# Two halves of a pair side by side: a bank for each spread and each transpose, two dT buffers, and the second correction at the turn's end

## What is computed

```python
summed = segment_sum(x[src], dst);  cnt = segment_sum(ones, dst)
aggr = summed / maximum(cnt, 1.0)[:, None]
h = aggr @ W_l.T + b_l + x @ W_r.T
mu, var = mean(h, axis=0), mean(square(h - mu), axis=0)
y = x + relu((h - mu) * rsqrt(var + EPS) * gamma + beta)
out = layernorm(y, axis=-1)
```

## Time and profile before

| | |
|---|---|
| median of 3 executions | 2656.01 us (2655.27 to 2657.59) |
| the profiled execution | 2652.04 us, of which its span 2650.3 us |
| PE busy | 1762.3 us (66%) |
| DVE busy | 1970.0 us (74%) |
| ACT busy | 1466.1 us (55%) |
| POOL busy | 1412.8 us (53%) |
| DMA over the span | 753.48 MB, mean 284 GB/s |

### The profile page before, as it was taken

How to read it: one execution, slowest core, us unless ns; L and a number is a source line. 1 busy time by engine, 2 the same in 40 slices (tenths; PEclk the granted TensorE clock), 3 DMA queues, 4 the chain that set the end, 5 groups by cost and what they waited for, 6 DMA issues and landing times.

```text
span 2650.3 us, 29633 instructions
## 1 busy us (share of the span) xinstructions
PE 1762.3 (66%) x9404; PEld 1421.6 (54%) x9404; DVE 1970.0 (74%) x3465; ACT 1466.1 (55%) x2847; POOL 1412.8 (53%) x688
## 2 busy tenths in 40 slices
PE   5589999999999999999999999997310000000000
PEld 4468777888887777888887777885200000000000
DVE  7735777788887777888887777885688766666666
ACT  3224444455555444555554444543369988888887
POOL 5334554545555555455555554554276656655554
PEclk9789999999999999999999999998655555555555
DMA  4256867888877877888877778888499999999998
GB/s 149 81 159 218 276 230 230 258 257 263 262 251 248 272 257 228 264 249 265 264 245 248 251 256 247 264 253 279 127 366 426 426 426 426 426 426 416 420 420 344
DMA packets 126763, 753.48 MB, mean 284 GB/s; under 512 B 22039, under 2 KB 22039, under 8 KB 66956
## 3 DMA queue, kind: packets, MB, share of 16 engines
q1 hardware_dynamic: 72940, 619.04, 60.7%
q0 software_dynamic: 53664, 132.51, 20.0%
HBM read 515.92 MB, written 246.22 MB: 288 GB/s over the span
## 4 chain that ended last, share of the span: by engine, by line
PE 49%; DMA 26%; DVE 11%; ACT 7%; issue 4%; POOL 2%; SPq 1%; DVEq 0%; POOLq 0%; ACTq 0%
DMA out<-hx 19%; PE pd L533 10%; PE pd L535 10%; PE pd L534 10%; PE pz L638 4%; PE pz L640 4%; PE pz L639 4%; DMA xf<-x,gi 4%; ACT hx L876 3%; ACT hx L886 2%; DVE x_lo L1032 2%; PE px L632 2%; DMA hs<-h_scratch 2%; DVE hot L1038 1%; PE pe L624 1%
## 5 line engine op out<-in xcount | busy, mean ns | idle before, releaser
L1368 POOL DMA_INDIRECT h_scratch<-zz,si x156 | 306.4, 1964 | 683.5 <-ACT zz L790 467.8
L533 PE MATMUL pd<-wc_hi,x_hi 128*128 128x512 f32 x1564 | 639.1, 409 | 40.8 <-POOL x_lo L1295 24.6
L534 PE MATMUL pd<-wc_lo,x_hi 128*128 128x512 f32 x1564 | 617.6, 395 | 7.0 <-issue 7.0
L535 PE MATMUL pd<-wc_hi,x_lo 128*128 128x512 f32 x1564 | 619.1, 396 | 0.0
L1391 POOL TENSOR_TENSOR hx<-hx,scale_b 128x2560 f32<-128x2560 f32 (+2 forms) x91 | 439.5, 4843 | 291.5 <-DMA hx<-h_scratch 250.0
L745 ACT ACTIVATE h_out<-pd 128x512 f32<-128x512 f32 x391 | 233.0, 596 | 403.5 <-PE pd L535 401.9
L533 PEld LDWEIGHTS pd<-wc_hi,x_hi 128*128 128x128 f32 x1564 | 298.3, 191 | 102.4 <-POOL x_lo L1295 24.6
L1320 POOL DMA_INDIRECT xn<-x,gi x156 | 310.3, 1989 | 47.7 <-issue 44.9
L534 PEld LDWEIGHTS pd<-wc_lo,x_hi 128*128 128x128 f32 x1564 | 298.8, 191 | 63.8 <-issue 7.3
L535 PEld LDWEIGHTS pd<-wc_hi,x_lo 128*128 128x128 f32 x1564 | 297.7, 190 | 66.0
L783 ACT ACTIVATE dT_hi<-px 128x512 fp32r<-128x512 f32 x156 | 93.3, 598 | 399.3 <-PE px L632 388.0
(11 more groups left out here) (214 smaller groups left out, 2939.3 us busy)
## 6 DMA issues: line engine op xcount, KB each, us to landing
raw<-xT_whole SPq DMA_DIRECT2D x78, 1280.0 KB
h_scratch<-h_out SPq DMA_DIRECT2D x78, 1280.0 KB
hs<-h_scratch SPq DMA_DIRECT2D x78, 1280.0 KB
hx<-x SPq DMA_DIRECT2D x78, 1280.0 KB, 20.6
hx<-h_scratch SPq DMA_DIRECT2D x77, 1280.0 KB, 15.4
out<-hx SPq DMA_DIRECT2D x77, 1280.0 KB, 18.1
xn<-x,gi POOLq DMA_INDIRECT x156
xf<-x,gi POOLq DMA_INDIRECT x156
```

What stands on the lines that cost most here:

```text
L533: pe.matmul(pd[i][0:n, :], hi, wc["hi"][:, kc, :], start=kc == 0, stop=False)
L534: pe.matmul(pd[i][0:n, :], hi, wc["lo"][:, kc, :], start=False, stop=False)
L535: last = pe.matmul(pd[i][0:n, :], lo, wc["hi"][:, kc, :], start=False, stop=kc == KC - 1)
L1368: pool.indirect_dma_start(out=h_dram[:, :], out_offset=by, in_=zz[:, h, :], in_offset=None, bounds_check=N + 2 * P - 1, oob_is_err=True, c ...
```

## The change

- The spread of half 1 goes to the bank `p6` and its transposes to `p7` (`spread_to`, `turned`); half 0 keeps `pe_` and `px`. `dT_hi` and `dT_lo` are there twice.
- The waits on what frees a bank or buffer now reach two halves back instead of one (`2 * u + h - 1` for `2 * u + h`, from pair 1 on). `correction` and `copy_z` keep theirs, since `pz` stays single.
- In PE's list both spreads, then both transposes, then both corrections stand together, spaced by tiles: the second correction is last in the turn, behind the fifth tile.
- ACT's list: `copy_z(u, 1)` stands at the head of the next turn; the copy of the fifth tile is in its own turn and not at the head of the next; the two `difference_high` stand behind the second and the third tile's copy; `copy_z(u, 0)` stands behind `extras_high`.
- DVE's list: both differences ahead of the squares, both `difference_low` behind them; `x_low` has five gaps instead of four. With t = 2 as the third tile of a turn it stood at the turn's end and now stands ahead of `take_sums`; as the fourth it stays at the end; as the fifth it stood behind `difference_low(p, 0)` of the next turn and now behind `difference(p, 0)`.

The number of instructions of each engine is the same.

```diff
         acc2 = sr("acc2", [P, TG, D], F32)
         hs = sr("hs", [P, 2, TG, D], F32)
-        dT_hi = sr("dT_hi", [P, KC, P], F32R)
-        dT_lo = sr("dT_lo", [P, KC, P], F32R)
+        dT_hi = [sr(f"dT_hi{h}", [P, KC, P], F32R) for h in range(2)]
+        dT_lo = [sr(f"dT_lo{h}", [P, KC, P], F32R) for h in range(2)]
...
         pe_, px, pz, psl, p6, p7 = (ps(n) for n in ("pe", "px", "pz", "psl", "p6", "p7"))
         banks = [(pe_, px), (pz, psl), (p6, p7)]
+
+        spread_to, turned = (pe_, p6), (px, p7)
         turn = [pe_, px, pz, psl, *pd]
...
                     pe.wait_ge(s_xel, u + 1)
                     pe.wait_ge(s_spread, u + 1)
-                if 2 * u + h > 0:
-                    pe.wait_ge(s_d, 2 * u + h)
+                if u > 0:
+                    pe.wait_ge(s_d, 2 * u + h - 1)
                 to = spread[:, h * P:(h + 1) * P]
-                pe.matmul(pe_[:], to, xe_hi[:], start=True, stop=False)
-                pe.matmul(pe_[:], to, xe_lo[:], start=False, stop=True).then_inc(s_e, 1)
+                pe.matmul(spread_to[h][:], to, xe_hi[:], start=True, stop=False)
+                pe.matmul(spread_to[h][:], to, xe_lo[:], start=False, stop=True).then_inc(s_e, 1)
             def transpose_difference(u, h):
                 pe.wait_ge(s_d, 2 * u + h + 1)
-                if 2 * u + h > 0:
-                    pe.wait_ge(s_dl, 2 * u + h)
+                if u > 0:
+                    pe.wait_ge(s_dl, 2 * u + h - 1)
                 for kc in range(KC):
-                    last = pe.transpose(px[:, kc * P:(kc + 1) * P], dd[:, h, kc * P:(kc + 1) * P], ident[:])
+                    last = pe.transpose(turned[h][:, kc * P:(kc + 1) * P], dd[:, h, kc * P:(kc + 1) * P], ident[:])
                 last.then_inc(s_x, 1)
-            def times_wl(out_bank, n):
+            def times_wl(out_bank, n, h=0):
                 for kc in range(KC):
-                    hi, lo = dT_hi[:, kc, 0:n], dT_lo[:, kc, 0:n]
+                    hi, lo = dT_hi[h][:, kc, 0:n], dT_lo[h][:, kc, 0:n]
                     pe.matmul(out_bank[0:n, :], hi, wl["hi"][:, kc, :], start=kc == 0, stop=False)
                     pe.matmul(out_bank[0:n, :], hi, wl["lo"][:, kc, :], start=False, stop=False)
...
                 if 2 * u + h > 0:
                     pe.wait_ge(s_ze, 2 * u + h)
-                times_wl(pz, P).then_inc(s_z, 1)
+                times_wl(pz, P, h).then_inc(s_z, 1)
             def sum_columns(m, acc, tiles):
...
                     plain(0)
                     if a is not None:
-                        transpose_difference(a, 0)
+                        spread_extras(a, 1)
                     plain(1)
                     if a is not None:
-                        correction(a, 0)
-                        spread_extras(a, 1)
+                        transpose_difference(a, 0)
                     plain(2)
                     if a is not None:
...
                     plain(3)
                     if a is not None:
-                        correction(a, 1)
+                        correction(a, 0)
+                    plain(4)
                     if u + 2 < U:
                         fill_slots(u + 2)
-                    plain(4)
+                    if a is not None:
+                        correction(a, 1)
                 pe.wait_ge(s_a1, G)
                 sum_columns(0, acc1, range(1, TG))
...
             def difference_high(u, h):
                 act.wait_ge(s_x, 2 * u + h + 1)
-                if 2 * u + h > 0:
-                    act.wait_ge(s_z, 2 * u + h)
-                act.activation(dT_hi[:].rearrange("p c r -> p (c r)"), px[:], ACT.Copy).then_inc(s_dh, 1)
+                if u > 0:
+                    act.wait_ge(s_z, 2 * u + h - 1)
+                act.activation(dT_hi[h][:].rearrange("p c r -> p (c r)"), turned[h][:], ACT.Copy).then_inc(s_dh, 1)
             def copy_z(u, h):
...
                                     x_high(g + 1, (g + 1) % 2, kc)
-                    plain(tiles_at(u - 1)[TG - 1:])
+                    if pair_at(u - 1) is not None:
+                        copy_z(u - 1, 1)
                     if sp_ is not None:
                         for t in range(3, tiles_in(sp_)):
                             square(sp_, t)
+                    plain(tiles[0:2])
                     if a is not None:
                         difference_high(a, 0)
-                    plain(tiles[0:2])
+                    plain(tiles[2:3])
+                    if a is not None:
+                        difference_high(a, 1)
+                    plain(tiles[3:4])
+                    if pair_at(u + 1) is not None:
+                        extras_high(u + 1)
                     if a is not None:
                         copy_z(a, 0)
-                        difference_high(a, 1)
-                    plain(tiles[2:4])
-                    if pair_at(u + 1) is not None:
-                        extras_high(u + 1)
+                    plain(tiles[4:])
                     if s is not None:
                         for t in range(min(3, tiles_in(s))):
                             square(s, t)
-                    if a is not None:
-                        copy_z(a, 1)
             act.wait_ge(s_bs, 1)
...
                 if u > 0:
                     dve.wait_ge(s_x, 2 * u + h - 1)
-                dve.tensor_tensor(dd[:, h, :], pe_[:], xf[:, u % 2, h, :], ALU.add).then_inc(s_d, 1)
+                dve.tensor_tensor(dd[:, h, :], spread_to[h][:], xf[:, u % 2, h, :], ALU.add).then_inc(s_d, 1)
             def difference_low(u, h):
                 dve.wait_ge(s_dh, 2 * u + h + 1)
-                if 2 * u + h > 0:
-                    dve.wait_ge(s_z, 2 * u + h)
-                dve.tensor_tensor(dT_lo[:].rearrange("p c r -> p (c r)"), px[:],
-                                  dT_hi[:].rearrange("p c r -> p (c r)").bitcast(F32), ALU.subtract).then_inc(s_dl, 1)
+                if u > 0:
+                    dve.wait_ge(s_z, 2 * u + h - 1)
+                dve.tensor_tensor(dT_lo[h][:].rearrange("p c r -> p (c r)"), turned[h][:],
+                                  dT_hi[h][:].rearrange("p c r -> p (c r)").bitcast(F32), ALU.subtract).then_inc(s_dl, 1)
             def take_sums(g):
...
                 for u in turns():
                     p = pair_at(u)
-                    low = lows(u, ((0, 1), (0, 2), (0, 3), (0, 3), (1, 0)))
+                    low = lows(u, ((0, 1), (0, 2), (0, 3), (0, 4), (1, 0)))
                     def x_lows(place):
...
                     if p is not None:
                         difference(p, 0)
+                    x_lows(0)
                     if 0 <= u + 2 < U:
                         one_hots(u + 2)
                     if p is not None:
-                        difference_low(p, 0)
-                    x_lows(0)
+                        difference(p, 1)
+                    x_lows(1)
                     if sums_at(u - 1) is not None:
                         take_squares(sums_at(u - 1))
-                    x_lows(1)
                     if p is not None:
-                        difference(p, 1)
+                        difference_low(p, 0)
                     x_lows(2)
                     if p is not None:
                         difference_low(p, 1)
+                    x_lows(3)
                     if sums_at(u) is not None:
                         take_sums(sums_at(u))
...
                         begin(u + 1, 0)
                         begin(u + 1, 1)
-                    x_lows(3)
+                    x_lows(4)
                     if 0 <= u + 2 < U:
                         indices(u + 2)
```

More of the change, by code:

```diff
@@ L817, in correct @@
                             act.wait_ge(s_c[5], TG * g + t)
-                        act.activation(dT_hi[:, :, 0:n], px[:].rearrange("p (c r) -> p c r", c=KC)[:, :, 0:n],
+                        act.activation(dT_hi[0][:, :, 0:n], px[:].rearrange("p (c r) -> p c r", c=KC)[:, :, 0:n],
                                        ACT.Copy).then_inc(s_c[3], 1)
@@ L1155, in correct @@
                         dve.wait_ge(s_c[3], TG * g + t + 1)
-                        dve.tensor_tensor(dT_lo[:, :, 0:m], px[:].rearrange("p (c r) -> p c r", c=KC)[:, :, 0:m],
-                                          dT_hi[:, :, 0:m].bitcast(F32), ALU.subtract).then_inc(s_c[4], 1)
+                        dve.tensor_tensor(dT_lo[0][:, :, 0:m], px[:].rearrange("p (c r) -> p c r", c=KC)[:, :, 0:m],
+                                          dT_hi[0][:, :, 0:m].bitcast(F32), ALU.subtract).then_inc(s_c[4], 1)
                         dve.wait_ge(s_c[5], TG * g + t + 1)
```

## The result

The changed kernel takes 2615.9 us (median of 4 executions, 2606.9 to 2618.4) against 2655.6: a ratio of 0.9845, 95% interval 0.982 to 0.987. That is 40 us less, where 65 were forecast; it lies in the range, but outside the 2585 to 2604 of the main case. The profiled execution took 2615.85 us, 36.2 less than that of before.

The account below looks back on a forecast made before the run. PE's stalls in the 75 turns, mostly from DVE delivering late, were taken as the bound: 74.1 - 11.4 + 5 = 67.7 us, 65 after leaving 3 for small gaps, from 2656.01 to 2591 us, range 2576 to 2622.

Parts of the forecast that it names:

- the range: Whole kernel: 2576 to 2622 us, meant for 8 in 10, including rival 4 (faster, 2579) and rival 1's better half.
- the main case: Whole kernel: DVE's lateness goes, for a time of 2585 to 2604 us; chance 0.58.
- The pool of 74.1 us and the floor: PE in the 75 turns: 74.1 us lost over turns of 21.6 us (five tiles) or 18.8 (four), the most to win.
- DVE's lateness in the third and fourth tile's turns: Turns with t = 2 third or fourth: DVE delivers `dd` late; all of the 74.1 us from this goes.
- The second banks and `dT` buffers cost nothing: PSUM banks and `dT` buffers: free, and without them the new order would stand still at the transposes of half 1.
- `pz` and ScalarE, 11.4 us: Turns of four tiles: correction 1 waits for `copy_z`, later when `raw` holds up ACT; 11.4 us lost, 5 to about 40.
- The drain, 5 us: After the last tile: earlier loads and halves running side by side save 5 us, from 0 to 6.5.
- POOL: the term that was mis-sized: Gathers behind the slipped scatter-add: last issued by 13.7, `begin` at 18; landing up to 5 us later costs nothing.
- Rival 2: Scatter-add at the turn's head delays gathers, `begin`, `indices` and `dd` 0: slower, 2680 us at 1.3 more; chance 0.06.
- `dd` 1 is still there at 8.2: DVE with t = 2 first, second or fifth: `x_low` moves the rest by 3.0, `dd` 1 still meeting its 9.6 deadline.
- rival 1: ACT's chain from `raw` through `copy_z` to correction 1 becomes the bound: 2619 us, anything from 2605 to 2640; chance 0.22.
- Rival 3: No change: banks gain nothing and the vanished gaps return as the new wait for `pz`, 2656 us; chance 0.04.

Follow-up runs that it names:

- e7: Kernel before the change with only `x_low` of a group whose t = 2 is the turn's third tile moved ahead of `take_sums`: 2628.7 us, ratio 0.9902.
- e3: Kernel before the change with the second banks, `dT` buffers and relaxed waits, in the old order on every engine: 2653.6 us, ratio 0.9999.
- e4: Changed kernel's order on every engine, but one bank and one `dT` buffer for each purpose and the old waits: 2838.7 us, ratio 1.0692.
- e2: Changed kernel with both gathers of a turn ahead of the scatter-add of half 1 on GpSimd: 2590.3 us, ratio 0.9763.
- e1: Changed kernel with `indices` (and `x_low` of the last gap) ahead of `begin` on VectorE: 2601.0 us, ratio 0.9803.
- e11: Changed kernel with one more gather at the head of each turn's gathers, into a buffer nobody reads: 2663.5 us, ratio 1.0031.

## Why the prediction was right, and where its size was off

- **The pool of 74.1 us and the floor.** Right. A turn without waits is 21.6 us after the change too, and no run went under it: the best is 9.9 us above in sum.
- **DVE's lateness in the third and fourth tile's turns.** Right: 55.3 us over the floor fell to 8.2. e7 shows the third's part by itself. That only these turns lose was not right: the fifth tile's held 14.4, nearly all in the three turns (11, 38, 65) that follow one of four tiles with `x_low` at its end, so the same lateness carried over.
- **"The second banks and `dT` buffers cost nothing"** and are needed by the order. Right: e3 0.9999, e4 1.0692.
- **`pz` and ScalarE, 11.4 us.** Right once the gathers are in time: the turns of four tiles are 11.6 us over the floor in e2. In the changed kernel they are 15.6.
- **The drain, 5 us.** 4.0 measured, but only 0.8 in e2; what decides it is open.
- **POOL: the term that was mis-sized.** The step reads: "A landing later than that, by up to 5 us, pushes only `dd` 0, which has as much room." The landing was later, 12.2 us after the start of the issue in the case shown and 9.8 in the median of the waits. I put 0 us for it, and it measured 30: 42.6 over the floor against 12.7 in e2. Rival 2 did price a late landing, but took a `raw` load's 8.5 us as a sign against it, while the trace of before had eight of these very gathers at 10.0 to 11.9. Two more things were missing. I gave DVE's list for the fifth and first tile as if it entered the turn on time ("`dd` 1 is still there at 8.2"), but `dd` 0 came 4.4 us into the turn shown and up to 6.5 in others, with `x_low` still ahead of `dd` 1. And lateness isn't paid once: `indices` behind `begin` carries it to the next turn's gathers. e1 (cut that link), e2 (start sooner) and e11 (start later) each move the time the way this asks, by -15, -26 and +48.
- **The rivals.** 2616 falls in the band of rival 1, ScalarE's chain, but not by its cause: PE waited 7.0 us in all for `zz`. The mechanism was that of rival 2, to which I gave 0.06 because I asked only when it would eat the whole gain, and not what it would cost part of the way. Rival 3 fell.
- **The range.** That it took the time in is partly luck: it reached up to 2622 to cover half of rival 1, and the time got there by another cause. The main case had the mechanism and its price right but for POOL, and without that term, in e2, the time is 2590 where 2591 was forecast. That near agreement is in part luck too, since the drain gave less there.

The sum corrected by this one term, 2591 + 30, is 2621, 5 over the measured time. The 30 is itself a measurement, so this shows only that no other large term is missing.

## What to carry to other kernels

When an edit moves a DMA on the queue that also issues the gathers, ask for each gather who waits for its landing and what stands behind that wait, above all whether the next gather's indices do: then it is a loop, and its length and not its room is to be compared with the turn. Look in the trace of before for the longest landing of that transfer, even if it seldom ended a wait there. A buffer that never ended a wait gains nothing alone (e3), and may still be what a better order needs (e4). Work without a deadline, as a scatter-add, belongs behind work that has one.

## What the runs showed of the hardware

The last gather of the timeline above took 3.03 us to issue, others 1.0 to 1.7. DVE was adding squares meanwhile, both inputs in SBUF:

```profile
524.93 2.81 DVE L1108 TENSOR_TENSOR acc<-acc,hs 128x2560 f32<-128x2560 f32 x1
```

That ended at 527.74, the gather's issue at 528.62, 0.9 later. In the changed kernel 105 of the 500 indirect DMAs between 200 and 1740 us took 2.5 us or more, and 67 of them ended 0.9 us after such an addition; before it was 58 of 88. The other way round it is sharper: each of the 87 indirect DMAs that began while such an addition had 1.1 us or more to run ended 0.87 to 1.5 us behind it, and none sooner; before it was 59 of 59. The Trainium skill, "SBUF — State Buffer", "Who interferes with whom", says that a VectorE instruction with two SBUF inputs contends with GpSimd's reads of SBUF. It also tells of a probe in which `tensor_tensor` did not stall a DMA, and infers that descriptor generation needs only the write interface of the shared ports, which `tensor_tensor` leaves free. These rows speak against that inference: the issue stood still until the addition was over. No run here took the addition away, so the cause is argued from the coincidence.

The landing was the other surprise: 12.2 us from the start of a gather of 256 KB to the first use, beside a load of `raw`, a store and a load of sums of 1280 KB each, issued between 521.91 and 527.83; its own issue was 3.0 of these. Which of them held it up no run tells.
